# Seven picks instead of six, gather tables of 22 and 21 slots, attention side work in pieces, and attention products by halves of the nodes

## The reference, cut to what matters

```python
def _L0(A, X, W, b):                    # S = 25
    scores = where(A != 0, -arange(N), -inf)
    vals, idx = top_k(scores, 25)       # the first 25 neighbours of each node
    agg = where(valid, X[idx], -inf).max(axis=2)
    agg = where(degree <= 25, maximum(agg, 0), agg)
    return relu(concat([X, agg]) @ W + b)

def _L1(h, adj, W, b, a):               # graph attention; _L2 is the same without b
    z = h @ W.T + b
    e = leaky_relu((z @ a1)[:, None] + (z @ a2)[None, :], 0.2)
    att = softmax(where(adj > 0, e, -9e15))
    return elu(att @ z)

def _L3(x, adj, att_W, W0, b0, W1, b1): # full attention, two steps
    att = softmax((x @ att_W) @ x.T / sqrt(128) + where(adj == 1, 0, -1000))
    for W, b in ((W0, b0), (W1, b1)):
        x = tanh(att @ (x @ W + b))
    return x
```

## Time and profile before

| | us |
|---|---|
| median of three runs | 3027.49 |
| the profiled execution | 3027.64 |
| its span, first to last instruction | 3025.9 |
| PE busy | 1667.7 (55%) |
| DVE busy | 1384.0 (46%) |
| POOL busy | 1312.7 (43%) |
| ACT busy | 851.0 (28%) |

### The profile page before, as it was taken

How to read it: one execution, slowest core, us unless ns; L and a number is a source line. 1 busy time by engine, 2 the same in 40 slices (tenths; PEclk the granted TensorE clock), 3 DMA queues, 4 the chain that set the end, 5 groups by cost and what they waited for, 6 DMA issues and landing times.

```text
span 3025.9 us, 28047 instructions
## 1 busy us (share of the span) xinstructions
PE 1667.7 (55%) x9039; PEld 1232.9 (41%) x9086; DVE 1384.0 (46%) x3476; ACT 851.0 (28%) x1456; POOL 1312.7 (43%) x1362
## 2 busy tenths in 40 slices
PE   2772664535656356363463645645546544547667
PEld 1551542424435245252452534424344333524555
DVE  3762563435535346253462434624446344443642
ACT  2111433114331233212342133321333214223123
POOL 5456434354353454434544445434444545254100
PEclk9986677766878567785677856778668776778789
DMA  3122112121131111211112211122112222012001
GB/s 103 35 66 57 45 39 88 42 67 47 39 94 48 53 53 40 88 48 52 53 41 86 58 45 51 55 73 60 47 46 62 71 62 64 21 52 59 29 15 35
DMA packets 79677, 165.45 MB, mean 55 GB/s; under 512 B 24478, under 2 KB 41771, under 8 KB 79531
## 3 DMA queue, kind: packets, MB, share of 16 engines
q0 software_dynamic: 42752, 87.64, 10.8%
q1 hardware_dynamic: 36778, 75.98, 7.6%
HBM read 159.33 MB, written 4.19 MB: 54 GB/s over the span
## 4 chain that ended last, share of the span: by engine, by line
another core or an unknown queue 34%; PE 29%; issue 13%; DVE 10%; ACT 8%; DVEq 3%; POOL 1%; DMA 1%; ACTq 0%; SPq 0%; POOLq 0%
PE big L816 6%; PE big L930 4%; PE side L913 3%; PE big L887 3%; DVEq L65 2%; PE big L897 2%; PE spare L730 2%; PE big L776 1%; DVE neg_max L1214 1%; ACT adj_less L468 1%; PE big L863 1%; DVE stats L1112 1%; DVE keys L1004 1%; ACT running L485 1%
## 5 line engine op out<-in xcount | busy, mean ns | idle before, releaser
L443 POOL DMA_INDIRECT gathered<-in_x_dram,rows x1336 | 1309.0, 980 | 1495.2 <-DVE pooled L1068 746.3
L816 PE MATMUL big<-values,probs_t 128*128 128x129 f32 x2048 | 277.7, 293 | 110.4 <-issue 110.2
L816 PEld LDWEIGHTS big<-values,probs_t 128*128 128x128 f32 x2048 | 266.0, 208 | 123.9 <-issue 118.9
L1066 DVE TENSOR_REDUCE pooled<-gathered 128x128 f32<-128x2816 f32 (+1 forms) x64 | 302.2, 4722 | 4.3 <-issue 2.9
L1214 DVE TENSOR_REDUCE neg_max<-big 128x1 f32<-128x1024 f32 x64 | 78.4, 1225 | 445.9 <-PE big L900 247.3
L730 PE MATMUL spare<-hot,x_part 128*128 128x512 f32 x864 | 251.4, 451 | 13.9 <-DVE hot L1095 12.5
L913 PE MATMUL side<-recip_diag,work 128*128 128x128 f32 x1024 | 145.4, 302 | 180.8 <-ACT probs_t L601 164.0
L913 PEld LDWEIGHTS side<-recip_diag,work 128*128 128x128 f32 x1024 | 139.3, 215 | 205.1 <-issue 189.5
L897 PE MATMUL big<-xt,row_gain 128*128 128x512 f32 x256 | 134.4, 651 | 154.4 <-ACT values L531 107.9
L730 PEld LDWEIGHTS spare<-hot,x_part 128*128 128x128 f32 x864 | 186.8, 221 | 62.5 <-issue 18.0
L1107 DVE TENSOR_TENSOR best_t<-best_t,spare 128x512 f32<-128x512 f32 x38 | 26.1, 688 | 350.1 <-remote 327.0
(11 more groups left out here) (176 smaller groups left out, 2643.3 us busy)
## 6 DMA issues: line engine op xcount, KB each, us to landing
adj_in<-in_adj_dram SPq DMA_DIRECT2D x128, 512.0 KB
gathered<-in_x_dram,rows POOLq DMA_INDIRECT x1336
xs<-in_x_dram SPq DMA_DIRECT2D x8, 512.0 KB
out_dram<-xs SPq DMA_DIRECT2D x8, 512.0 KB
w_sb<-in_L_gnn_W_dram SPq DMA_DIRECT2D x1, 128.0 KB
w_sb<-in_L_gnn_W_dram SPq DMA_DIRECT2D x2, 64.0 KB
probs_t<-in_L_gnn_W_dram SPq DMA_DIRECT2D x1, 64.0 KB
gat_w<-in_L_gnn_W_dram SPq DMA_DIRECT2D x1, 64.0 KB
```

The lines of the kernel that those rows point to most:

```text
L443: rows_gathered[t % RING].raised_by(pool.indirect_dma_start(out=gathered[:, t % RING, k * C:(k + 1) * C], out_offset=None, in_=x_rows, in_ ...
L816: last = nc.tensor.matmul(heads[:, t, 0:C + 1], probs_t[:, j, t * P:(t + 1) * P], values[:, j, :], start=False, stop=(j == T - 1), skip_gr ...
L1066: link(nc.vector.tensor_reduce(pooled[:, t, :], gathered[:, t % RING, 0:n * C].rearrange("p (k c) -> p c k", k=n), AX.X, ALU.max))
```

## The change

1. `GATHERED = (22, 21)`: tiles 0 to 3 still have 22 gathered slots, tiles 4 to 7 have 21. The second half of the nodes therefore has four picked slots, and a graph seven picks. ACT makes `hot` of 0, 1, 2, 5, 6 and DVE that of 3 and 4 (`BY_DVE`).
2. Pick 4 moves from behind the first step of layer 3 to the middle of its logits (before `t == 2`), and its `hot` is made before the pooling of the step `attention`. Pick 5 takes the old place of pick 4, pick 6 that of pick 5. ACT makes `hot` 5 before the first tanh and `hot` 6 before the second.
3. In `SIDE`, pooling tile 3 moves from the step `attention` into two halves of the features behind `t = 2` and `t = 3`, and `find_members` of the last pair, which was one piece behind `t = 3`, becomes three pieces behind `t = 4, 5, 6`.
4. In `gat`, PE first multiplies all eight source tiles for target tiles 0 to 3, then all for 4 to 7; the counts of layer 2 stand in the second half. DVE takes the first half's reciprocals, then does its side work, then adds the first half, and goes on with the second.
5. Among the 24 picks of graph 0 all eight poolings have a place (two stood behind the picks), the lists and the turning for graph 1 come earlier, and the count of the second half goes through two banks beside pick 11.
6. In the last graph the last tile is pooled in two parts, the first before its last six gathers are waited for.

The core of the diff:

```diff
-GATHERED = 22
+GATHERED = (22, 21)
+LATE = 6
+PICKED = (SAMPLES - GATHERED[0], SAMPLES - GATHERED[1])
+PICKS = PICKED[0] + PICKED[1]
+BY_DVE = (PICKED[0], PICKED[0] + 1)
-FIRST_POOL = {3: 0, 7: 1, 11: 2, 15: 3, 19: 4, 23: 5}
-FIRST_LISTS = 16
-FIRST_FEEDS = {13: 0, 17: 1}
+FIRST_POOL = {3: 0, 7: 1, 10: 2, 12: 3, 14: 4, 17: 5, 20: 6, 23: 7}
+FIRST_LISTS = 11
+FIRST_FEEDS = {7: 0, 13: 1}
-        "attention": [("pool", 1, 2), ("pool", 1, 3)],
-        "tile 3": [("members", 1, 3)],
+        "attention": [("pool", 1, 2)],
+        "tile 2": [("pool a", 1, 3)],
+        "tile 3": [("pool b", 1, 3)],
+        "tile 4": [("members a", 1, 3)],
+        "tile 5": [("members b", 1, 3)],
+        "tile 6": [("members c", 1, 3)],
...
 def gather(b, t):                                    (POOL)
-                for k in range(gathered_slots(b)):
+                for k in range(gathered_slots(b, t)):
...
 def graph(b, slot, in_loop):                         (ACT)
+                if exists(b, 1, B, in_loop):
+                    make_hot(b + 1, 5)
                 for h in range(2):
                     act.wait_ge(att_heads.sem, att_heads.at(b, h + 1))
                     att_tanh.raised_by(nc.scalar.activation(xt[:, halves[h]], low[:, halves[h]], ACT.Tanh))
                 take_xw(b, 1, high_t)
                 feed(b, slot, 3, 0, in_loop)
+                if exists(b, 1, B, in_loop):
+                    make_hot(b + 1, 6)
...
 def gat(b, slot, layer, in_loop):                    (PE)
-                for j in range(T):
-                    pe.wait_ge(gat_probs.sem, gat_probs.at(b, l * T + j + 1))
-                    for t in range(T):
+                for h in range(2):
+                    for j in range(T):
+                        if h == 0:
+                            pe.wait_ge(gat_probs.sem, gat_probs.at(b, l * T + j + 1))
+                        for t in range(HALF * h, HALF * h + HALF):
...
-                    if layer == 2 and j >= HALF and exists(b, 1, B, in_loop):
-                        if j == HALF:
-                            spare_maxed(b + 1, 2)
-                        for k in range(2 * (j - HALF), 2 * (j - HALF) + 2):
-                            count(b + 1, 1 - slot, 1, k)
+                        if layer == 2 and h == 1 and exists(b, 1, B, in_loop):
+                            if j == 0:
+                                spare_maxed(b + 1, 2)
+                            count(b + 1, 1 - slot, 1, j)
...
 def graph(b, slot, in_loop):                         (PE)
                 for t in range(T + 2):
+                    if t == 2 and exists(b, 1, B, in_loop):
+                        spare_maxed(b + 1, 3)
+                        pick(b + 1, 4)
...
 def gat(b, slot, layer, in_loop):                    (DVE)
-                side_work(b, slot, f"gat {layer} heads", in_loop)
-                for t in range(0, T, 2):
-                    dve.wait_ge(gat_heads.sem, gat_heads.at(b, (l * T + t) // 2 + 1))
-                    gat_recip.raised_by(nc.vector.reciprocal(recip[:, t:t + 2], heads[:, t:t + 2, C]))
-                if picks and layer == 2:
-                    make_hot(b + 1, 3)
-                for h in range(2):
...
+                take_heads(range(0, HALF, 2))
+                side_work(b, slot, f"gat {layer} heads", in_loop)
+                add_heads(0)
+                take_heads(range(HALF, T, 2))
+                if picks and layer == 2:
+                    make_hot(b + 1, 3)
+                add_heads(1)
                 layer_norm(slot)
...
-            for t in range(len(FIRST_POOL), T):
-                pool_tile(0, 0, t)
```

More of the change, by code:

```diff
@@ L713, in count_first, with pick_tiles @@
-                    count_psum.raised_by(nc.tensor.matmul(bank, count_through[:, :], adj_t[slot][:, j, halves[0]],
-                                                          start=(j == 0), stop=(j >= T - 2), skip_group_check=True))
+                    count_in_two(b, slot, 0, j)
+            def pick_tiles(b, q, tiles):
+                per = T // CHUNKS
+                for m in tiles:
+                    c = m // per
+                    if m % per == 0:
+                        if isinstance(b, int) and b == 0:
+                            pe.wait_ge(hot_ready.sem, hot_ready.at(b, CHUNKS * q + c + 1))
+                        elif q in BY_DVE:
+                            pe.wait_ge(hot_ready.sem, hot_ready.at(b, CHUNKS * (q - BY_DVE[0]) + c + 1))
+                        else:
+                            pe.wait_ge(hot_made.sem, hot_made.at(b, CHUNKS * (q - (q > BY_DVE[1]) * len(BY_DVE)) + c + 1))
+                    for part in range(X_PARTS):
+                        last = nc.tensor.matmul(pick_bank(b, q), x_parts[part][:, m, :], hot[c][:, m % per, :],
+                                                start=(m == 0 and part == 0),
+                                                stop=(m == T - 1 and part == X_PARTS - 1))
+                    if m % per == per - 1:
+                        hot_used.raised_by(last)
```

238 lines of the change are left out of this document (146 added, 92 removed).

## The result

The changed kernel took 3061.30 us (median of 4 runs, 3026.2 to 3068.12), the kernel before 3022.09 (3003.64 to 3029.78) beside it: 1.0091 times the time, 95% interval 1.0047 to 1.0135. (The ratios in this text are the measured ones, with their intervals; they are not quotients of the medians, which here would be 1.013.) I had forecast 2979, and 2915 to 3060 as the range: the median lies 1.3 us above its upper end. The profiled execution took 3058.45 us.

What follows compares the result with a forecast made beforehand. Unbroken gather runs were taken to stop PE and all that waits for it. Terms summed to -4.9 us a graph, -34 over seven graphs, and -15 at the start: 3027.6 to 2979 us, forecast's own range 2950 to 3010, outer 2915 to 3060.

Steps and rivals of the forecast that it cites:

- Heads by halves: GAT heads: layer 1 gathers 6 to 7 us later, mostly absorbed, +2; layer 2 -1.5; together +0.5 us a graph.
- first rival: Halves put DVE's side work behind PE, so POOL starts later and stops end later: about 3060 us; chance 0.18.
- second rival: Gathers do not matter; something else stops PE: 3042 us, or 3030 with a hidden pick; chance 0.09.
- Gathers: POOL, tiles 4 to 7: 28 gathers fewer at 1.25 us, 35 us in all, -5.0 us a graph.
- Seventh pick: PE, layer 3 logits: 16 more matmuls a graph cost +3.9 us, ends 0 and +7.2.
- Side work in pieces: `find_members` cut in three: PE's 2.57 us wait for `recip_diag` goes, -2.3 us a graph.
- Tiles 6 and 7 in one run: Their gathers merge into one 53 us run, stopping PE once instead of twice: 0 a graph, ends -8 and +8.
- `hot` 4 ahead of the pooling: DVE work before the pooling of `attention` breaks the run of tiles 4 and 5: -2 us a graph.
- The start: Graph 0's picks: the 44 gathers behind them begin about 20 us earlier, shortening the 52 us stop: -15 us.
- The reading of what bounds the kernel: About 10 us into an unbroken gather run PE nearly stops, until about 4 us behind the last gather.
- the third: A rival: one stop of 17 us a graph goes away altogether, 2910 us or so; chance 0.12.
- the fourth: A rival: POOL waits anyway in the steady state, so only the start gains: 3012 us; chance 0.11.

Runs made afterwards that it cites:

- stopping condition: Run sets, like the prediction's own, in which PE stops during gathers; in the later ones the kernel before took 3049 and 3058 us.
- free condition: Four later run sets in which the kernel before took 1978 to 1979 us; its trace has no such stops of PE.
- set IV: Changed kernel without halves and pieces, six picks: with 22 gathers everywhere 1955.82 us (0.9884 of the kernel before), with 22 and 21 gathers 1925.16 us (0.9726).
- the paced runs: Four unused semaphore increments on POOL behind each gather: in the changed kernel 2935.50 us (0.9653), in that without halves and pieces 2917.44 us (0.9511).
- sets IV to VI: Changed kernel with gather counts, seventh pick, halves or pieces altered, or with semaphore increments behind gathers: 0.9726 to 0.9884, then 0.9653 to 1.0054, then 0.9511 and 0.9801.

## Why the prediction was wrong

**The step that failed is "Heads by halves".** I had the delay right (6.6 us behind PE's return, gathers 6 to 7 us later) and then wrote that PE's work runs on and arrives at the next stop further ahead, and left +2 and together +0.5 a graph. Undoing this one part in the stopping condition gives 62 us, or 9 a graph by the period (377.5 - 368.1). PE does not arrive further ahead: when the run's last gather is out it has done the same 56 matmuls behind layer 1's products with the delay as without it. The run ends as much later, and the pooling behind it too. That is my first rival, with its 6.6 and 3.4 us standing nearly in full (9 of 10 a graph). Its reason against, "a later start leaves PE unstopped for as long", is true and worth nothing: PE spends the time waiting, 9.88 us where it had waited 3.75, because ACT's and so PE's next work hangs on the second half's reciprocals, and I had put these behind the very side work that starts 6.6 us later. The sum left that wait out altogether. How much of the 62 us comes by the later gathers and how much by PE's own longer waits (120 us in all against 76) no run separates; both come from the one delay. In the free condition the same part costs 18 us (halves alone) to 24 (undone in the changed kernel), where POOL's wait for `pooled` grows by 19 us while POOL is itself the bound.

The rival's number is partly luck. Its 3060 is called the price "when half of the delays is caught up", but half of 15 us gives 3027.6 + 7 x (-3.4 + 7.5) - 15 = 3041; 3059 comes out with the 10 us in full and the later list of tile 6 at nothing. The second rival has a slip too: with a hidden pick it is 3027.6 + 7 x (-2.3 + 0.5) = 3015, not 3030.

**The rest of the sum comes out as a whole, and partly by luck.** Without halves the change gives 0.9858 (0.9779 to 0.9936) in the stopping condition; the forecast, without its +0.5, is 0.983. But the terms do not stand one by one: the start and the pieces gained nothing that I can see, and the pick, priced at +27 us in all, cost nothing where it was measured. By terms:

- Gathers, -35 us: 28 of them are 31 us in the free condition (set IV), and about 38 in the stopping one (0.9801 against 0.9677, across sets, intervals touching, so a rough figure). Right.
- Seventh pick, +3.9 a graph: nothing in the free condition; not measured apart in the other one. Its lower end, 0, is what the runs support, in the free condition alone.
- Side work in pieces, -2.3: not seen. Undone beside the halves it changes nothing in the free condition (0.9731 and 0.9722); undone with the halves in place, 0.9852 becomes 0.9796, 11 us faster (another chip). PE's wait for `recip_diag`, which I took from one graph, is 7.3 us in three places over the whole trace of the kernel before, and none after:

```profile
PE side L913 <- DVE recip_diag L1221: 7.3, 3, 2.6
```

- Tiles 6 and 7 in one run, 0: the merging came as said, and its cost is open between 0 and +6 a graph. The merging of tiles 0 and 1 I had missed.
- `hot` 4 ahead of the pooling, -2: not tried alone.
- The start, -15: wrong. The gathers behind the picks start no earlier (234.10 against 234.83 us), and graph 1's tile 4 starts at 438.24 us against 426.62, 428.88 without the halves; in the free condition the start is worth 0 to 12 us. The waiting only moved, ahead of the run before.

**The reading of what bounds the kernel** was right for the traces that I had, and incomplete: that PE's stops belong to gather runs showed in each stopping trace, and the paced runs show that breaks in a run go with PE's return (122 us less in all). But gather runs alone do not stop PE: the free traces have the same gathers, 1.25 us apart, 77 in 100 us, and no stop. Nor is it plainly PE that stops. The copy of ACT's that is released at 1288.26 waits for these products, the last of their kind before the stop:

```profile
1265.41 2.02 PE L913 MATMUL side<-recip_diag,work 128*128 128x128 f32 x16 [0.21 <-ACT probs_t L601]
```

By the profile, whose ends of matmuls are modelled, they were over at 1267.43; ACT hears of them 20.8 us later, and PE waits for ACT. What is late there is the release. In the stop ahead of the earlier trace rows it is PE itself: its matmuls come singly, one in 1.4 to 2.1 us, and their waits are put to "issue".

By the Trainium skill, "SBUF — State Buffer", section "SBUF: two separate sides", PE never waits on anyone, and the engines' side and the DMAs' side cannot contend; the free traces agree (538 matmuls beside 77 gathers), the stopping ones do not (3 beside 11), so what stops PE there is not shown to be the access to SBUF, and no run here names it.

The second rival (gathers do not matter) fell with sets IV to VI, the third (a stop goes away) and the fourth (only the start gains) with the profile after.

## What to carry to other kernels

Where one engine's transfers stop another and a third frees their buffers, the work that frees the buffer goes first, and so does the work that the next engine waits for: a cut of PE's products into halves that puts buffer-freeing work behind the first half cost 9 us a graph for a tail shortened by an estimated 3. A delay is free only if the other engines have work of their own to fill it, and that is read from the stretches and waits, not assumed. And before a kernel is tuned on one trace, time it in a second set of runs: the same change was worth +0.9% here and -1.5% there.

## What the hardware showed that I had not expected

- One kernel, one chip, two conditions: the kernel before took 1979 and 3049 us on chip 4, the variant without halves 1927 and 2996. The two traces of that variant, both from chip 4, have the same matmuls, PE busy for 1554 and 1698 us and POOL for 1310 and 1283. The difference is engines standing still during gathers.
- In the stopping condition breaks in the gather runs, 195 us of them in 1308 gathers, took 4% off the changed kernel (1.0054 to 0.9653) and 3% off the variant without halves and pieces (0.9801 to 0.9511).
- With a memset (0.33 us) and a drain of POOL behind each indirect DMA, POOL waits 2.0 us ahead of the next one instead of 0.3, and a gather comes every 3.3 us instead of 1.25.
- PE's granted clock is lower in the traces in which PE stands still more: 0.75 to 0.77 over the span in the stopping ones, 0.87 to 0.91 in the free ones, and 0.66 in the one with the drain.
